# One transformer stack on one core: the top-32 mask is put ahead of the exponent, two small copies go

## The reference, cut to what matters

```python
scores = jnp.einsum('bhqa,bhka->bhqk', q, k) * SCALE
top_vals = jax.lax.top_k(scores, TOP_K)[0]          # TOP_K = 32
cutoff = top_vals[..., -1:]
masked = jnp.where(scores >= cutoff, scores, -jnp.inf)
w = jax.nn.softmax(masked, axis=-1)
e = jnp.einsum('bhqk,bhka->bhqa', w, v)
```

## Time and profile of the kernel before

| | |
|---|---|
| three runs | 545.12, 541.65, 537.23 us |
| span of the profiled execution | 543.1 us |
| busy: PE, DVE, ACT, POOL | 471.0, 477.4, 294.5, 263.8 us |

### The profile page before, as it was taken

One profiled execution on the slowest core, in us unless ns is written; L12 is line 12 of the kernel. 1 busy time (PEld: TensorE's weight loads), 2 busy tenths in 40 slices (PEclk: granted clock), 3 DMA queues, 4 the chain that ended last, 5 costly groups with the idle time before them and its releaser, 6 DMA issues. The chain is left out here.

```text
span 543.1 us, 12113 instructions
## 1 busy us (share of the span) xinstructions
PE 471.0 (87%) x3161; PEld 347.3 (64%) x3161; DVE 477.4 (88%) x3011; ACT 294.5 (54%) x812; POOL 263.8 (49%) x403
## 2 busy tenths in 40 slices
PE   4999999898986999799889898999889989689485
PEld 3578877566755765467657666667657757566374
DVE  5784679959879899899989999999999999999972
ACT  1143551433444335424777788787786887635343
POOL 4320120500323435634685687777668667736622
PEclk9999999979998999899999999999999998989957
DMA  8700000000000000000000000000000000000000
GB/s 278 301 2 1 2 1 2 0 1 0 2 2 0 2 2 1 1 1 2 7 1 8 7 2 2 10 2 2 11 1 2 7 7 7 2 5 8 6 5 11
DMA packets 5938, 9.68 MB, mean 18 GB/s; under 512 B 744, under 2 KB 4976, under 8 KB 5616
## 3 DMA queue, kind: packets, MB, share of 16 engines
q1 hardware_dynamic: 5584, 8.35, 4.3%
q10 hardware_dynamic: 288, 0.56, 0.3%
HBM read 7.86 MB, written 1.05 MB: 16 GB/s over the span
## 5 line engine op out<-in xcount | busy, mean ns | idle before, releaser
L1318 PE MATMUL psT<-mrow,mones 128*128 128x308 bf16 x840 | 131.3, 303 | 5.0 <-ACT vv L672 4.3
L939 DVE MAX8 top<-area_b 128x8 f32<-128x77 f32 x768 | 116.0, 290 | 0.0
L1318 PEld LDWEIGHTS psT<-mrow,mones 128*128 128x128 bf16 x840 | 83.6, 101 | 41.2 <-issue 14.7
L947 DVE MATCH_REPLACE8 area_b<-top,area_b 128x77 f32<-128x77 f32 x512 | 109.1, 293 | 0.0
L947 DVE MATCH_VALUE_LOAD area_b<-top,area_b 128x8 f32 x512 | 74.2, 150 | 0.0
L947 DVE MATCH_REPLACE8 area_b<-top,area_a 128x77 f32<-128x77 f32 x256 | 54.7, 286 | 0.0
L1088 PE MATMUL psM<-vblk,pT 128*128 128x135 f32 (+3 forms) x320 | 42.4, 288 | 5.2 <-ACT early L562 3.0
L1088 PEld LDWEIGHTS psM<-vblk,pT 128*128 128x128 f32 (+1 forms) x320 | 39.7, 197 | 8.9 <-issue 7.2
L420 POOL TENSOR_TENSOR p<-area_b 128x1232 f32<-128x1232 f32 x15 | 41.9, 2792 | 6.9 <-issue 3.3
L1286 PE MATMUL psM<-vblk,pT 128*128 128x135 f32 (+3 forms) x320 | 43.5, 292 | 1.5 <-ACT pT L631 0.8
L1286 PEld LDWEIGHTS psM<-vblk,pT 128*128 128x128 f32 (+1 forms) x320 | 41.2, 203 | 5.1 <-issue 4.3
(11 more groups left out here) (223 smaller groups left out, 1015.0 us busy)
## 6 DMA issues: line engine op xcount, KB each, us to landing
area_a<-in_w1T SPq DMA_DIRECT2D x1, 2064.0 KB, 11.0
area_b<-in_w SPq DMA_DIRECT2D x1, 2048.0 KB, 15.4
x<-in_x SPq DMA_DIRECT2D x4, 256.0 KB, 6.9
out<-fin SPq DMA_DIRECT2D x16, 64.0 KB, 1.5
rows<-in_rows SPq DMA_DIRECT2D x1, 576.0 KB, 6.7
vblk<-in_vblk SPq DMA_DIRECT2D x1, 540.0 KB, 15.6
weights<-in_weights SPq DMA_DIRECT2D x1, 516.0 KB, 6.5
consts<-in_consts ACTq DMA_DIRECT2D x1, 392.5 KB, 3.9
```

What stands on the lines that cost most here:

```text
L939: ins = e.max(tops[:, r, h], (left if r else scores_sb[t % RING])[:, h])
L947: ins = e.match_replace(left[:, h], tops[:, r, h], (left if r else scores_sb[t % RING])[:, h], GONE)
L1318: mm(bank[:, 0:B * KEYS], mones[:], mrow.rearrange("p b k -> p (b k)"), start=True, stop=True)
```

## The change

In layer 1, for tiles 0 to 14, the mask is now subtracted ahead of the exponent: `drop` is one Relu of -1e30 times `cut` (0 where the score is kept, a huge number where it isn't), `fall` on POOL subtracts it from `dif` in place, and `exp` on ACT writes straight into `p1`, which PE turns. The Sign pass and the constant `tiny` go, and so does the product on POOL. `exp` stands right behind `fall` in the list, `dif` right ahead of the `cut` of its own tile. `dif` of a tile now waits until the exp of the tile before is done. Tile 15 keeps its way. The copies `load` and `keys` go: PE and ACT read `yg` and `kblk1` in place. The rest of the list is as it was.

```diff
-                e.tensor_copy(cur[:], yg[:, t, :]).then_inc(s["cur_set"], 1)
-                e.tensor_copy(kcur[:], kblk1.rearrange("p b i k -> p b (i k)")[:, t // NJ]).then_inc(s["kcur_set"], 1)
                 def a():
                     hold(e, s["topk_step"], TOPK_STEPS * t + G)
-                    hold(e, s["exp_set"], t)
+                    hold(e, s["p_set"], t)
                     e.tensor_tensor(dif[:], scores_sb[t % RING][:], ...)
                 def b():
                     hold(e, s["dif_set"], t + 1)
-                    hold(e, s["p_set"], t)
+                    hold(e, s["fall_set"], t)
                 def c():
-                    hold(e, s["exp_set"], t + 1)
                     hold(e, s["keep_set"], t + 1)
-                    hold(e, s["p_turned"], 3 * t)
-                    e.tensor_tensor(p1.rearrange("p (h k) -> p h k", k=KEYS), ex1, cut, ALU.mult).then_inc(s["p_set"], 1)
+                    e.tensor_tensor(dif[:], dif[:], cut, ALU.subtract).then_inc(s["fall_set"], 1)
...
                 def a():
-                    hold(e, s["dif_set"], t + 1)
-                    hold(e, s["p_set"], t)
-                    e.activation(ex1, dif[:], ACT.Exp, scale=SCALE).then_inc(s["exp_set"], 1)
+                    if t < LASTT:
+                        hold(e, s["fall_set"], t + 1)
+                        hold(e, s["p_turned"], 3 * t)
+                        e.activation(p1.rearrange("p (h k) -> p h k", k=KEYS), dif[:], ACT.Exp, scale=SCALE).then_inc(s["p_set"], 1)
+                    else:
+                        hold(e, s["dif_set"], t + 1)
+                        e.activation(ex1, dif[:], ACT.Exp, scale=SCALE).then_inc(s["exp_set"], 1)
                 def b():
                     hold(e, s["cut_set"], t + 1)
-                    e.activation(cut, cut, ACT.Sign, bias=tiny[:]).then_inc(s["sign_set"], 1)
-                    hold(e, s["sign_set"], t + 1)
-                    e.activation(cut, cut, ACT.Relu).then_inc(s["keep_set"], 1)
+                    e.activation(cut, cut, ACT.Relu, scale=DROP).then_inc(s["keep_set"], 1)
...
                 def turn():
-                    hold(e, s["cur_set"], t + 1)
+                    hold(e, s["gates_set"], min(t + 1, NJ))
-                    tr(psM0[:, 0:P], cur[:, 0:D], ident)
+                    tr(psM0[:, 0:P], yg[:, t, 0:D], ident)
...
-                    hold(e, s["kcur_set"], t + 1)
+                    hold(e, s["kblk1_made"], B)
```

More of the change, by code:

```diff
@@ L47 @@
 GONE = -3.0e38
-TINY = 1e-30
+DROP = -1.0e30
 F32 = mybir.dt.float32
@@ L638, in weigh @@
                 if t < LASTT:
-                    steps.update(sign=b)
+                    steps.update(drop=b)
                 return steps
@@ L957, in f @@
                     def f():
-                        hold(e, s["exp_set"], t + 1)
+                        hold(e, s["exp_set"], 1)
                         hold(e, s["p_turned"], 3 * t)
@@ L1402 @@
-fill@218 scores@5 max31@4 copy2@3 scale2@6 max32@4 value@3 keep@5 max33@4 keys@6 cut@4 norm2@6 max00@5 max01@5 turn@7 max02@5 copy@7
-max03@5 fill@219 fill@220 moe0@7 affine@6 sign@4 mark00@5 dif@5 mark01@5 mark02@5 gated0@7 norm@3 mark03@5 product@4 acopy@3
-fill@221 fill@222 fill@223 fill@224 fill@225 fill@226 fill@227 fill@228 moe1@7 sum3@6 max10@5 square3@6 max11@5 gated1@7 max12@5
-max13@5 fill@229 fill@230 fill@231 fill@232 moe2@7 aproduct@3 mark10@5 gated2@7 turn0@4 add3@3 exp@5 total@7 mark11@5 scale3@6
@@ L1434 @@
-norm3@11 mark21@9 copy1@8 lturn@11 turn2@8 lT@11 mark22@9 gated1@12 up@7 mark23@9 ask@11 acts@7 moe2@12 max30@9 qT@11 half@7 down@7
-gated2@12 max31@9 scores@11 copy2@8 max32@9 fvalue@7 total@12 keys@12 max33@9 keep@11 max00@10 cut@9 max01@10 max02@10 value@8
-max03@10 sum2@12 square2@12 mark00@10 load@13 sign@9 dif@10 mark01@10 mark02@10 mark03@10 scale2@12 max10@10 product@9 norm2@12
-norm@8 max11@10 acopy@8 fill@305 fill@306 fill@307 fill@308 fill@309 fill@310 fill@311 fill@312 turn@13 max12@10 copy@13 max13@10
@@ L1442 @@
-max32@10 copy2@9 scores@12 max33@10 norm2@13 acts@8 max00@11 affine@13 value@9 keep@12 max01@11 half@8 max02@11 cut@10 sum3@13
-max03@11 square3@13 mark00@11 down@8 turn@14 copy@14 mark01@11 fvalue@8 scale3@13 sign@10 moe0@14 mark02@11 dif@11 mark03@11 norm@9
-max10@11 acopy@9 gated0@14 max11@11 aproduct@9 max12@11 add3@9 norm3@13 fill@322 fill@323 fill@324 fill@325 fill@326 fill@327
-fill@328 fill@329 moe1@14 max13@11 keys@13 sum4@9 mark10@11 product@10 lturn@13 gated1@14 mark11@11 square4@9 fill@330 fill@331
@@ new lines @@
+fill@217 moe2@6 max23@4 norm3@5 turn1@3 gated2@6 mark20@4 lturn@5 lT@5 total@6 copy1@3 mark21@4 mark22@4 mark23@4 turn2@3 ask@5
+sum2@6 qT@5 max30@4 square2@6 fill@218 scores@5 max31@4 copy2@3 scale2@6 max32@4 value@3 keep@5 max33@4 dif@4 cut@4 norm2@6
+max00@5 max01@5 turn@7 max02@5 copy@7 max03@5 fill@219 fill@220 moe0@7 affine@6 drop@4 mark00@5 mark01@5 mark02@5 gated0@7
+norm@3 mark03@5 fall@4 exp@4 acopy@3 fill@221 fill@222 fill@223 fill@224 fill@225 fill@226 fill@227 fill@228 moe1@7 sum3@6
@@ new lines @@
+half@4 down@4 copy1@5 mark20@6 affine@8 turn@9 copy@9 turn2@5 mark21@6 copy2@5 moe0@9 sum3@8 fvalue@4 mark22@6 square3@8 end@4
+value@5 gated0@9 mark23@6 scale3@8 max30@6 max31@6 norm3@8 max32@6 moe1@9 max33@6 lturn@8 lT@8 max00@7 dif@6 cut@6 gated1@9
+max01@7 fill@246 ask@8 max02@7 qT@8 fill@247 fill@248 fill@249 scores@8 max03@7 mark00@7 drop@6 moe2@9 mark01@7 mark02@7
+mark03@7 gated2@9 keep@8 fall@6 exp@6 fill@250 fill@251 fill@252 fill@253 fill@254 fill@255 fill@256 total@9 max10@7 max11@7
@@ new lines @@
+copy1@9 max31@10 scale2@13 ask@12 qT@12 turn2@9 max32@10 copy2@9 scores@12 max33@10 norm2@13 acts@8 max00@11 affine@13 value@9
+keep@12 max01@11 half@8 max02@11 dif@10 cut@10 sum3@13 max03@11 square3@13 mark00@11 down@8 turn@14 copy@14 mark01@11 fvalue@8
+scale3@13 drop@10 moe0@14 mark02@11 mark03@11 norm@9 max10@11 acopy@9 gated0@14 max11@11 aproduct@9 max12@11 add3@9 norm3@13
+fill@322 fill@323 fill@324 fill@325 fill@326 fill@327 fill@328 fill@329 moe1@14 max13@11 sum4@9 mark10@11 fall@10 exp@10
```

284 lines of the change are left out of this document (138 added, 146 removed).

## The result

The changed kernel took 580.21 us (median of 4 runs, 577.19 to 582.97), the kernel before 543.24 beside it; the ratio is 1.0718 (1.0664 to 1.0772). The direction was forecast and the time lies in the range, but the step is 37 us where the forecast had 26. Four later batches of the kernel before, run beside the experiments, have medians of 540.5 to 542.2 us (7 to 23 runs each), so the step is rather 38 to 40 us.

The account below looks back on a forecast made before the run. DVE paces the middle, with a POOL-ACT-PE loop beside it nearly a second bound; terms 3.6 + 2.3 + 3.8 + 8.4 + 5.1 + 6.6 - 3.7 = 26.1 us gave 569.2 us of span, 567.8 us predicted, range 551 to 582.

Parts of the forecast that it names:

- rival C: PE's clock falls more often after longer idle at each turn; 3 us at five more tiles, 583 us; chance 0.09.
- the credit of 3.7 us for the copies: `load` and `keys` leave POOL, 0.74 us a tile, credited at five tiles where POOL itself is late: -3.7 us.
- the 0 for tiles 0 to 3: POOL idle ahead of `cut` and `dif`; removed sign and moved `exp` about cancel: 0 us.
- The second loop beside DVE: Per-tile path over POOL, ACT and PE from `cut` to next `cut`; one or two us of room in 19, nearly a bound.
- Rival A: DVE hides the loop and only tile 14's 6.6 us are paid, about 548 us; chance 0.16.
- rival B: Not slower: shorter ACT queue, DVE's 5.0 us of waits disappear, about 537 to 541 us; chance 0.07.
- the 30 that were named as the sign: Expected evidence: ACT's largest wait is `exp` for POOL's fall, some 2.5 us nearly every tile, 30 us or more in all.
- the dear part: `exp` right behind `drop` waits for the fall; what ACT queued behind waits 2.79 + 1.23 us more.
- The three prices worked out from rows: Delays of ACT's work behind `exp`: +3.6 us at tile 5, +2.3 at tile 9, +3.8 at tile 10.
- dif ahead of cut: `dif`'s 2.25 us on POOL, hidden before, now delay `cut` wherever POOL does not stand waiting for DVE.
- Tiles 4 to 13: Worked prices at 5, 9, 10; 2.1 us each at 4, 11, 12, 13; +5.1 for 6 to 8.
- The tail: Tile 14: tile 15's `dif` and `exp` wait for tile 14's `exp`, delaying the first copy; +6.6 us, counted in full.

Follow-up runs that it names:

- e5: Changed kernel with 121 more warm-up steps on PE at ten places where PE stood after tile 4; 572.78 us, ratio 1.0544 to the kernel before.
- e4: Kernel before with only the copies `load` and `keys` taken out; 540.23 us, ratio 0.9984.
- e1: Changed kernel with `exp` of tiles 0 to 13 up to four steps later in ACT's queue; 555.95 us, ratio 1.0270 to the kernel before.
- e2b: Changed kernel with `dif` of tiles 1 to 14 earlier in POOL's queue, `exp` left behind the fall, run again for its trace; 568.72 us, ratio 1.0495.
- e3: Changed kernel with both `exp` later in ACT's queue and `dif` earlier in POOL's queue; 554.70 us, ratio 1.0249 to the kernel before.
- e8: Changed kernel with two arrays for `dif`, so it stands between `cut` and `fall` again, `exp` left right behind the fall; 583.06 us, ratio 1.0691.
- e6: Kernel before with `dif` moved ahead of its own tile's `cut` and `exp` ahead of the sign; 573.48 us, ratio 1.0571.
- e11: e6 without the sign pass on ACT, so kept weights are multiplied by their distance to the cutoff; 544.46 us, ratio 1.0031 to the kernel before.
- e13: Kernel before without the copies, with 24 more warm-up steps on PE ahead of the turn of tile 14; 542.50 us, ratio 1.0009.

## Where the forecast was right, and the step that failed

**The step that failed.** The path was right, the sum was too small: 26.1 us of span, where the two profiles differ by 32.3 (by 35.0 from `cut` of tile 0 on) and the medians by 37 to 40. The step that failed is the price of nothing for PE's clock: rival C was set beside the forecast, and no term of the sum held it, while e5, which only fills PE's new stops, gets some 7 us back, about the 6.2 by which the profiled spans miss the sum. Two smaller terms were off as well: the credit of 3.7 us for the copies, of which e4 shows 0.9 in the kernel before, and the 0 for tiles 0 to 3, which cost about 3.

**What bounds.** Right. The second loop beside DVE was nearly a bound, and the change put it over: DVE waits at line 960 and the delay grows from tile 4 on. Rival A (DVE hides it, 548 us) and rival B (ACT has enough else to do, 537 to 541) fall: ACT waits 34.9 us at `exp`, more than the 30 that were named as the sign.

**exp, "the dear part".** Right, and shown by e1: 24 of some 39 us come back when only `exp` is moved back in ACT's queue. The three prices worked out from rows were met in the stretches that they were worked out for. At tile 9 it is 2.28 us for 2.3 (above). The scalings behind `exp` at tiles 5 and 10 begin after the change at

```profile
346.87 0.35 ACT L566 ACTIVATE mparts<-psM,yg 128x128 f32<-128x128 f32 x1
...
457.29 1.12 ACT L566 ACTIVATE mparts<-psM,yg 128x128 f32<-128x128 f32 x4
```

which is 9.90 and 11.06 us behind POOL's turn to the tile (336.97 and 446.23), and 3.7 and 3.9 us more than before, for 3.6 and 3.8.

**dif ahead of cut.** Right in kind, and the price is not a fixed one. I wrote 2.25 us a tile less the room. Undone in the changed kernel it gives 12 us (e2b), undone with `exp` late hardly one more (e3 over e1), undone with `exp` in place by way of the shade nothing (e8), and done in the kernel before, with `exp` ahead of the sign, it costs 31 (e6). Adding up per-tile prices was the weak step of the method: the loop has a threshold (e11), so the prices depend on what else is in it.

**The copies.** Not borne out. "I credit 0.74 us at five tiles" was worth 0.9 us in all in the kernel before, which is not told from nothing (e4); in the changed kernel it was not tried. The row that I had before me said so: POOL stood 16.5 and 10.2 us at these copies for PE. Where a copy did hold up `cut`, at tile 9 (from 407.09 to 408.74, `keys`), its end was already in that tile's price. That is up to 3.7 us of the shortfall.

**Tiles 4 to 13.** By the table 27.2 us where the sum had 23.2. Tile 4, for which I took a middle of 2.1, cost 3.5; tiles 5 to 7 together 7.4 for 5.5; tiles 8 and 9 together 5.5 for 5.5; tile 10 3.8 for 3.8; tiles 11 to 13 together 7.0 for 6.3. The middle taken for tiles without rows of their own was too low at tiles 4, 12 and 13 (3.5, 2.9 and 2.6 us) and too high at tile 11 (1.5). PE's clock alone is large enough for the 4.0 us: from `cut` of tile 4 to that of tile 14 it is 222.0 us in the changed kernel and 217.3 in e5.

**The tail.** The mechanism and its size at the first copy are right (+6.73 for the 6.6 forecast; "about 17 us" was 17.24). But only 4.6 us reached the end. The products with the values of tile 14 ran at a granted clock of 0.50 before (522.60 to 527.20) and at 1.00 now (556.80 to 559.50). Two stretches, the kernel before and then the changed one; PE's granted clock is the third number from the end:

```profile
522.60:527.20 4.60, 4.60 (x21) 4.29 (x20) 1.86 (x10) 0.28 (x1) 0.99 (x2) 0.50 0.05 14
```

```profile
556.80:559.50 2.70, 2.62 (x22) 2.38 (x20) 2.00 (x11) 0.28 (x1) 1.01 (x2) 1.00 0.04 12
```

Two us of the 6.7 came back there; no term of the sum stood for that.

**Rival C.** Set beside the forecast as another way in which it could go, at 0.09, and priced at nothing in the sum. It is not another way but an addition: the new stops at 343.0 and 385.6 us were followed by four us at a mean granted clock of 0.57 and 0.63, and e5 gets 7.4 us back with ACT's waits at `exp` and the mask as they were. The measured 580.2 us lie nearer to rival C's 583 than to 567.8, but C asked for 15 us of clock, twice what e5 gives. No run shows its 3 us at each of five more tiles, which were an estimate; the runs showed 7.4 us in their place, for ten filled stops together. This was the largest step missed: the earlier trace rows has PE at a granted clock of 0.54 behind a stop, so the new stops had to be priced. The changed kernel bears that out in part: of the thirteen stops over 1.2 us that it shows behind 180 us, nine have a mean granted clock of 0.50 to 0.71 over the 4 us behind them, the shortest of them 2.2 us long (276.1 to 278.3, then 0.64), while one of 3.0 us (322.1 to 325.1) has 1.00.

**The sum and the medians.** 26.1 forecast, plus 3.7 (copies), plus 4.0 (tiles 4 to 13), less 2.0 (tail), plus 0.5 (tiles 0 to 3: about 3 less the 2.7 by which `cut` of tile 0 came sooner) is 32.3, the difference of the two spans. The credit is booked whole here, though what the copies are worth in the changed kernel is open. The medians differ by 5 to 7 us more, since the profiled execution of the kernel before (543.1 of span, some 545 in all) was above its medians, and that of the changed kernel (577.19) 3.0 below its own. The base was not the error: 541.65 lies among the later medians of the kernel before.

**What stays open.** e5's 7.4 us are measured with `exp` and `dif` in place; how much clock is in the 24 us of e1 or the 31 of e6 was not separated. What the copies would cost in the changed kernel, what a higher clock is worth where the loop has room, and why tiles 0 to 3 cost about 3 us is open too.

## What to carry to other kernels

Before a step is moved behind a wait in an engine's in-order queue, list what stands behind it there: the wait is paid by all of that, not by the step (24 of some 39 us here, e1). Here a loop beside the pacing engine, with one or two us of room, cost next to nothing until it was full; then a 1.33 us pass cost 2 us a tile (e11). So find the room first, and don't add up prices of steps one by one. A step hidden in another's shade (here `dif` under the mask) has a place worth keeping, and new stops of PE should be priced twice where the trace shows a lower clock behind them, once for the wait and once for that clock (here 0.57 behind the stop at tile 8, and some 7 us in all, e5).

## What the runs showed of the hardware

PE's clock: the stops of 4.2, 3.5 and 2.5 us at 343.0, 385.6 and 428.8 in the changed kernel were followed by four us at a mean granted clock of 0.57 (shown with e5), 0.63 and 0.71, the one of 3.0 us at 322.1 by four us at 1.00 (length, PE busy, granted clock, DMA):

```profile
389.06:393.06 4.00, 4.00 (x23) 0.63 0.00 0
431.34:435.34 4.00, 4.00 (x17) 0.71 0.00 0
325.13:329.13 4.00, 3.97 (x31) 1.00 0.02 4
```

With warm-up steps in the stops the place at tile 8 stayed at 1.00, and some 7 of 580 us came back. One stop filled in the kernel before without the copies raised the mean granted clock of the 7.1 us behind it from 0.55 to 0.76, that of four us later on was 0.50 where it had been 0.65, and nothing was won (542.50 us for 540.23, e13).
